# Joint value steps of two key tiles, head parts laid by two transfers each in another order, and less fill, in a two-layer decoder kernel

## The reference

```python
x = x + _L0_attn_ref(_layernorm(x), ...)                        # "own": causal, 1024 keys, keys and values gated
x = x + _L0_xattn_ref(_layernorm(x), ctx_1024, ctx_1024, ...)   # "cross": rotary, causal mask, 154 keys
x = x + _L0_ffn_ref(_layernorm(x), ...)
x = x + _L1_attn_ref(_layernorm(x), ...)                        # "second": no mask, 1024 keys
x = x + _L1_xattn_ref(_layernorm(x), ctx_1024, ctx_1024, ...)   # one wide head, 154 keys
x = x + _L1_ffn_ref(_layernorm(x), ...)                         # 16 experts

scores = jnp.einsum('bhqd,bhkd->bhqk', q, k) / jnp.sqrt(d)      # inside each of the 16-head attentions
w = jax.nn.softmax(scores, axis=-1)
out = jnp.einsum('bhqk,bhkd->bhqd', w, v)
```

## Time and profile before

| | before |
| --- | --- |
| median of 3 runs | 3350.33 us (3348.94 to 3357.76) |
| the profiled execution | 3356.7 us, its span 3355.1 us |
| mean granted clock of PE | 0.996 of full |
| PE busy | 3191.1 us, 95% |
| DVE / ACT / POOL busy | 2323.0 (69%) / 1782.8 (53%) / 634.7 us (19%) |
| transfers | 147.74 MB, mean 44 GB/s |

### The profile page before, as it was taken

The page is one execution under the profiler, slowest core; times in us unless marked ns, Lnnn a source line. Parts: engine busy times, 40 slices in busy tenths (PEclk is TensorE's granted clock), DMA queues, the critical chain, the costliest instruction groups (busy, mean ns, idle before and its releaser), DMA issues.

```text
span 3355.1 us, 46975 instructions
## 1 busy us (share of the span) xinstructions
PE 3191.1 (95%) x17720; PEld 1713.3 (51%) x17720; DVE 2323.0 (69%) x4331; ACT 1782.8 (53%) x2551; POOL 634.7 (19%) x1166
## 2 busy tenths in 40 slices
PE   6999889999999989999999998999999999899999
PEld 4444433378644443337864444334786444433477
DVE  7856688556685578856678557885667855788555
ACT  3565546643456555664355555566424655556632
POOL 0322010024132201012403120100340321020033
PEclk9999999999999999999999999999999999999999
DMA  3212011023121202111312020120231202021023
GB/s 138 51 34 39 1 34 34 11 65 114 32 52 26 40 1 38 30 35 53 115 38 43 18 40 1 39 39 25 63 105 42 40 17 39 5 44 30 10 84 96
DMA packets 118101, 147.74 MB, mean 44 GB/s; under 512 B 25384, under 2 KB 75920, under 8 KB 117596
## 3 DMA queue, kind: packets, MB, share of 16 engines
q1 hardware_dynamic: 117876, 144.74, 18.1%
HBM read 74.25 MB, written 4.46 MB: 23 GB/s over the span
## 4 chain that ended last, share of the span: by engine, by line
PE 51%; DVE 8%; ACT 4%; issue 2%; DMA 1%; SPq 1%; POOL 0%; DVEq 0%; ACTq 0%
PE psum L1908 13%; PE psum L708 9%; PE psum L674 8%; PE psum L646 7%; PE psum L1000 4%; DVE small L796 3%; ACT work L756 2%; PE psum L939 1%; PE psum L717 1%; PE psum L500 1%; DMA work<-work 1%; PE psum L481 1%; PE psum L929 1%; SPq L863 1%; PE psum L1734 1%
## 5 line engine op out<-in xcount | busy, mean ns | idle before, releaser
L796 DVE TENSOR_REDUCE small<-psum 128x1 f32<-128x512 f32 (+6 forms) x1856 | 1136.7, 656 | 210.2 <-PE psum L646 175.9
L756 ACT ACTIVATE work<-psum 128x1024 f32<-128x1024 f32 (+5 forms) x1024 | 918.3, 935 | 419.4 <-PE psum L674 317.4
L646 PE MATMUL psum<-work 96*128 96x512 bf16 (+4 forms) x2688 | 655.7, 308 | 32.8 <-DVE small L796 16.2
L1908 PE MATMUL psum<-rounded_work 128*128 128x512 f32 x2592 | 602.0, 394 | 9.9 <-DVE rounded_work L1994 6.5
L674 PE MATMUL psum<-work 99*128 99x512 bf16 (+4 forms) x2048 | 564.2, 358 | 6.9 <-ACT work L756 4.0
L1908 PEld LDWEIGHTS psum<-rounded_work 128*128 128x128 f32 x2592 | 489.9, 190 | 116.0 <-DVE rounded_work L1994 8.3
L708 PE MATMUL psum<-work 128*32 128x512 f32 (+4 forms) x4480 | 532.3, 528 | 1.6 <-ACT work L756 1.4
L646 PEld LDWEIGHTS psum<-work 96*128 96x128 bf16 x2688 | 233.5, 97 | 544.4 <-DVE small L796 332.2
L674 PEld LDWEIGHTS psum<-work 99*128 99x128 bf16 (+1 forms) x2048 | 178.5, 97 | 199.3 <-ACT work L756 63.1
L2009 ACT CAST rounded_work<-work 128x512 fp32r<-128x512 f32 x144 | 89.4, 621 | 344.5 <-DVE work L2050 321.7
L846 POOL CAST small<-small 128x16 bf16<-128x16 f32 x96 | 18.8, 196 | 1156.2 <-DVE small L803 586.8
(11 more groups left out here) (297 smaller groups left out, 3765.2 us busy)
## 6 DMA issues: line engine op xcount, KB each, us to landing
work<-work SPq DMA_DIRECT2D x320, 192.0 KB, 4.3
work<-combine SPq DMA_DIRECT2D x64, 512.0 KB, 4.1
work<-in_w_gate SPq DMA_DIRECT2D x64, 128.0 KB, 3.5
work<-in_w_up SPq DMA_DIRECT2D x64, 128.0 KB, 3.5
work<-in_w_down SPq DMA_DIRECT2D x64, 128.0 KB, 3.8
work<-in_x SPq DMA_DIRECT2D x8, 512.0 KB, 4.9
out<-x SPq DMA_DIRECT2D x8, 512.0 KB, 2.9
work<-work SPq DMA_DIRECT2D x64, 28.9 KB, 2.0
```

The costliest lines, as they stand in the source:

```text
L646: ins = nc.tensor.matmul(dst[:, c * n:(c + 1) * n], A.q_pair[0:ROWS, slot, h, P * i:P * (i + 1)], A.k_of(pair, h)[0:ROWS, s0:s0 + n], star ...
L756: nc.scalar.activation(probs[0:size, n % 4, :, 0:P * many], banks(2 * (n % 2), 2)[0:size, :, 0:P * many], ACT.Exp, scale=DH ** -0.5).then_ ...
L796: nc.vector.tensor_reduce(tops[:, pair % 2, places[0]:places[-1] + 1:step], src, AX.X, ALU.max) \
L1908: ins = nc.tensor.matmul(dst, a_parts[i], b_parts[j], start=start and n == 0, stop=stop and n == 2, skip_group_check=True)
```

## The change

It has four parts. (a) Values are emitted two key tiles at a time, and there are six `probs` buffers in place of four. (b) A head's stack is laid by two transfers of 48 rows each: one of the three high parts (for the queries read three times from one part), one of the rest; so a stack has one copied part instead of three, the copies move from DVE to ACT and POOL, and a half whose parts are ready may go before the other. Context keys are laid pair by pair like the others, in front of the queries of that pair. (c) Fill is 14 and 2 in place of 26 and 9, and the second stage's ring waits for a unit of its own per bank. (d) `wide_q` is no longer resident; it is loaded in the second stage ahead of pair 6's top transfer.

```diff
+PROBS = 6
-    def value(pair, s):
-        pieces = [("value", pair, s)]
-        if s == len(steps) - 1:
+    def values(pair, s):
+        pieces = [("value", pair, s), ("value", pair, s + 1)]
+        if s + 1 == len(steps) - 1:
...
-            while sum(len(steps[later]) for _, later in held[1:]) >= 2:
-                value(*held.pop(0))
-    for which in held:
-        value(*which)
+            while sum(len(steps[later]) for _, later in held[2:]) >= 2:
+                values(*held[0])
+                held = held[2:]
+    for which in held[::2]:
+        values(*which)
...
-        probs = area.take(4, 2, HALF)
+        probs = area.take(PROBS, 2, HALF)
...
-                by, n, had = {}, 0, [None] * 3
+                by, n, had = {}, 0, [("second_rest", 4 + j) if self.tag == "second" else None for j in range(3)]
...
-        def load_queries(A, pair):
+        UPPER = 3 * DH
+        def load_queries(A, pair, low=None):
...
-                nc.sync.dma_start(A.q_pair[0:ROWS, slot, h, :], q_cut[r + DH * h:r + DH * (h + 1), :, k, :]) \
-                    .then_inc(*up(LOADED[2 * slot + h], A.tag, pair, by=16))
+                src, dst = q_cut[r + DH * h:r + DH * (h + 1), :, k, :], A.q_pair[:, slot, h, :]
+                if low is not True:
+                    nc.sync.dma_start(dst[0:UPPER, :], spread(src[:, Q_HIGH], 1, 3)).then_inc(*up(LOADED[2 * slot + h], A.tag, pair, by=16))
+                if low is not False:
+                    nc.sync.dma_start(dst[UPPER:ROWS, :], src[:, Q_MIDDLE:Q_LOW + 1]).then_inc(*up(LOADED[2 * slot + h], A.tag, pair, by=16))
...
+                for low in (False, True):
+                    keys_ready(0, low)
+                    load_keys(A, 0, low)
+                if a == "cross":
+                    for pair in (1, 2):
+                        load_keys(A, pair)
+                for low in (False, True):
+                    queries_ready(0, low)
+                    load_queries(A, 0, low)
+                for pair in range(1, A.slots):
+                    if pair == 4:
+                        keys_ready(1)
+                        queries_ready(1)
+                    if a == "second" or pair > 2:
+                        load_keys(A, pair)
                     load_queries(A, pair)
...
+                    if a == "second" and pair == PAIRS_OF_HEADS - 2:
+                        for loaded in range(PAIRS_OF_HEADS - SLOTS, PAIRS_OF_HEADS):
+                            for h in range(2):
+                                sp.wait_ge(*at(LOADED[2 * (loaded % SLOTS) + h], a, loaded))
+                        nc.sync.dma_start(wide_q, io["wide_q"]).then_inc(*up("wide_q_landed", by=16))
...
-                nc.sync.dma_start(ctx_stacks[0:ROWS, head, :], ctx_cut[r:r + DH, :, k, :]).then_inc(*up("context_keys_landed", by=16))
...
-            cross_doubles(0)
             cross_rest(3)
-            cross_doubles(1)
...
-            dve.wait_ge(*at("second_rest", "cut", 3))
-            double_queries(nc.vector, 0, "first_doubled", "q", 0)
...
-            busy_tensor(9, 0)
+            busy_tensor(2, 0)
...
-            busy_tensor(26, cross_banks[0])
+            busy_tensor(14, cross_banks[0])
```

More of the change, by code:

```diff
@@ L501, in project @@
             return ins
+        Q_MIDDLE, Q_MIDDLE_TOO, Q_LOW, Q_HIGH = range(4)
+        K_LOW, K_MIDDLE, K_HIGH, K_HIGH_TOO = range(4)
         area = Area(work, words)
@@ L560, in build_program @@
         wide_v = area.take(2, D)
+        wide_q = area.take(KD, D)
         area.at = WIDE_AT
@@ L624, in heads_tensor @@
             a, ring = A.tag, A.ring()
-            entered(pe)
-            busy_tensor(wait, 7)
+            if entered:
+                entered(pe)
+                busy_tensor(wait, 7)
             def take(*piece):
@@ L696, in heads_tensor @@
                                 i0, _, many = A.steps[s][part]
-                                moving = probs[0:size, A.number[(pair, s, part)] % 4, h, 0:P * many]
+                                moving = probs[0:size, A.number[(pair, s, part)] % PROBS, h, 0:P * many]
                                 dst = bank(7)[rows, P * (i0 // 2):P * (i0 // 2 + many)]
@@ L753, in heads_scalar @@
                     act.wait_ge(*at("scored", a, n))
-                    if n >= 4:
-                        act.wait_ge(*at("valued", a, *A.order[n - 4][0:2]))
-                    nc.scalar.activation(probs[0:size, n % 4, :, 0:P * many], banks(2 * (n % 2), 2)[0:size, :, 0:P * many],
+                    if n >= PROBS:
+                        act.wait_ge(*at("valued", a, *A.order[n - PROBS][0:2]))
+                    nc.scalar.activation(probs[0:size, n % PROBS, :, 0:P * many], banks(2 * (n % 2), 2)[0:size, :, 0:P * many],
                                          ACT.Exp, scale=DH ** -0.5).then_inc(*up("prob", a, n))
@@ L854, in heads_gpsimd, with load_keys @@
                     gate_values(key[1])
[L855 to L856 removed]
                 elif kind == "context":
                     context_gpsimd(*key)
[L860 removed]
+        UPPER = 3 * DH
+        def load_queries(A, pair, low=None):
             k, r, slot = pair // 4, 2 * DH * (pair % 4), pair % A.slots
             for h in range(2):
[L863 to L866 removed]
+                src, dst = q_cut[r + DH * h:r + DH * (h + 1), :, k, :], A.q_pair[:, slot, h, :]
[3 more added lines that the diff above has]
+                    nc.sync.dma_start(dst[UPPER:ROWS, :], src[:, Q_MIDDLE:Q_LOW + 1]).then_inc(*up(LOADED[2 * slot + h], A.tag, pair, by=16))
+        def load_keys(A, pair, low=None):
             k, r, slot = pair // 4, 2 * DH * (pair % 4), pair % A.slots
+            cut = ctx_cut if A.tag == "cross" else k_cut
             for h in range(2):
[L869 to L870 removed]
+                src, dst = cut[r + DH * h:r + DH * (h + 1), :, k, :], A.k_of(pair, h)
+                if low is not True:
+                    nc.sync.dma_start(dst[UPPER:ROWS, :], src[:, K_MIDDLE:K_HIGH_TOO + 1]).then_inc(*up(LOADED[2 * slot + h], A.tag, pair, by=16))
+                if low is not False:
+                    nc.sync.dma_start(dst[0:UPPER, :], src[:, K_LOW:K_HIGH + 1]).then_inc(*up(LOADED[2 * slot + h], A.tag, pair, by=16))
         def minus_ones(tag):
@@ L1638, in second_gpsimd @@
             for n, (name, k, half) in enumerate(second_units):
-                if n < 4:
-                    continue
                 _, _, cut, rest, parts = second_parts[name]
-                pool.wait_ge(*at("first_doubled", "q", 0))
-                pool.wait_ge(*at("second_middle", n))
-                nc.gpsimd.tensor_tensor(half_of(cut[:, parts[2]], k, half), raw_half(rest, k, half), half_of(cut[:, parts[1]], k, half), ALU.subtract) \
-                    .then_inc(*up("second_cut", n))
@@ L1661, in second_banks_free @@
-        def second_banks_free(queue):
-            queue.wait_ge(*at("second_rest", 6))
+                if n >= 4:
+                    pool.wait_ge(*at("second_rest", "cut", 3))
+                    pool.wait_ge(*at("second_middle", n))
+                    nc.gpsimd.tensor_tensor(half_of(cut[:, parts[2]], k, half), raw_half(rest, k, half), half_of(cut[:, parts[1]], k, half), ALU.subtract) \
+                        .then_inc(*up("second_cut", n))
+                if name == "k":
+                    pool.wait_ge(*at("second_high", n))
+                    high_again(k_cut, 2 * k + half, "second")
+                else:
+                    pool.wait_ge(*at("second_middle", n))
+                    middle_again(2 * k + half, "second")
@@ new lines, in second_queries, with second_keys @@
+        def second_queries(k, low=True):
+            if low:
+                sp.wait_ge(*(at("second_cut", 7) if k else at("second_rest", "cut", 3)))
+                sp.wait_ge(*at("part_again", "second", "q", 2 * k + 1))
+            else:
+                sp.wait_ge(*at("second_high", 4 * k + 3))
+        def second_keys(k, low=True):
+            sp.wait_ge(*at("part_again", "second", "k", 2 * k + 1))
+            if low:
+                sp.wait_ge(*(at("second_cut", 5) if k else at("second_rest", "cut", 1)))
+            else:
+                sp.wait_ge(*at("second_middle", 4 * k + 1))
```

166 lines of the change are left out of this document (67 added, 99 removed).

## The result

The changed kernel takes 3452.61 us (median of 4 runs, 3445.02 to 3459.0), the kernel before 3353.89 in the same runs (4, 3348.94 to 3357.76): a ratio of 1.0294, with a 95% interval of 1.0266 to 1.0323. That is 99 us slower. 58 us slower was forecast, with a range that ended at 3445, so the sign was right and the size was not. The profiled execution is the fastest of the four; their granted clocks fall as their times rise (0.984, 0.982, 0.981 and 0.978 for 3445.0, 3449.7, 3455.5 and 3459.0 us), so the trace shows less of the clock's part than the median has.

A forecast was written before the change was run, and what follows sets the result against it. PE was taken to bound the kernel, busy 3191.1 of 3355.1 us. Own stage -3.0, cross +7.0 and second stage +10.5 gave +14.5 us a trip, +58 for four: 3408 us, range 3388 to 3435 (0.8 between 3343 and 3445).

The forecast's parts named there:

- cross entry: Before the first cross score: half-stack issues on SP's queue make it +3 us later a trip, bounds -3 to +7.7.
- the cross stage behind it: After the first cross score: +1.7 us a trip for extra issues at pairs 6 and 7, +2.3 for later tops.
- own stage: Own stage: joint values save 7.3 us, stalls, tail and entry take some back; net -3.0 a trip, bounds -7.3 and +1.
- the second stage's entry: Entry of the second stage: copies leave DVE and half stacks go early, -2.4 us a trip, bounds -3 and 0.
- a rival of 0.13: Whole kernel: more idle PE lowers its clock, or both unknowns lie at their upper ends; 3435 to 3470 us, chance 0.13.
- I take 0.53 and 0.45: SP's queue before the first cross score: assumed us per query half and small key half, 17.1 us for 34 issues.
- the upper end: Cross entry: if a half costs 0.65 us whatever its size, 34 take 22.1 and the first score moves +7.7.
- Second stage: Second stage: stalls after double value blocks +8.1 us, tail +2.9, entry -2.4, wide_q +1.9; +10.5 a trip.
- The 3.02 us from top to score: Second stage: time from a top to a score needing its rows; the plan leaves 2.1, so the top's cycle grows 0.83.
- the recurrence: Second stage: hand-worked double cycle in which first passes wait for DVE's maxima; 5.85 us, not 5.43, +0.18 against now.
- wide_q: Second stage: the 256 KB wide_q transfer ahead of the last but one top costs +1.9 us a trip.
- the first passes wait for DVE over 100 us: Sign in the changed profile: first passes wait for DVE over 100 us in all instead of 16.2.

The follow-up runs named there:

- e5: The changed kernel with 60 fill matmuls in place of 10 ahead of the first cross score; 3424.8 us, 1.0207 of the kernel before.
- e1: The changed kernel with the context keys of pairs 3 to 5 issued early, with those of pairs 1 and 2; 3414.1 us, 1.0173 of the kernel before.
- e8: The changed kernel with the upper query halves of cross pairs 1 and 2 laid by three transfers of 16 rows in place of one of 48; 3463.0 us, one run.
- e3: The changed kernel with value steps one key tile at a time as before; 3392.6 us, 1.0110 of the kernel before.
- e7: The changed kernel with DVE's maxima in the second stage taken over half of each block's columns; 3411.6 us, one run.
- e12: The changed kernel with both DVE's maxima and ACT's exponentials halved in the second stage; 3379.2 us, one run.
- e9: The changed kernel with the fill of before, 26 and 9 matmuls in place of 14 and 2; 3453.9 us, 1.0283 of the kernel before.
- e2: The changed kernel with context keys of pairs 3 to 5 early and queries of pairs 4 and 5 behind tops 0 and 1; 3390.1 us, 1.0101 of the kernel before.
- e6: The changed kernel with each top three first passes into the next pair in place of four; 3514.2 us, one run.

## Why the prediction was wrong in size

Against the sum's terms the two traces have, in us a trip, +4.2 at the cross entry, +4.3 in the cross stage behind it, +2.7 in the own stage, +0.5 at the second stage's entry, -3.0 in the second stage and -1 in the rest: +31 in all, to which the medians add some 10.

- **The clock: the step that failed.** The sum has the wait before the first cross score and nothing for what the clock does behind it. That stood apart, as a rival of 0.13 whose range, 3435 to 3470, is where the result came. The evidence for leaving it out was a window in which PE waited a little at each first pass and kept its clock; this wait was of another kind, 10.8 us without any work, and PE ran at half clock for 23, 16, 4 and 16 us behind it. e5, which fills the wait and changes nothing else, gave 28 us back and came to 3424.8, inside the forecast's range. My text had a wait of some 5 us there and said that it is more than any now; by e1, where waits of 2.6 to 3.5 us were enough, that wait had to have its price too. In the stretch behind the first cross score, where the sum had +4, e5's three trips at full clock show +2.4 to +2.8 and the changed kernel's mean is +8.1.
- **Cross entry: a term mis-sized.** "I take 0.53 and 0.45" for the issues of a half: they are 0.635 each, and e8 has the same for 16 rows. With it the sum gives 21.6 and the upper end, which is what came: +7.2 for +3, 17 us in all. I had reasoned from bytes and rows; the row of the context stacks, 0.65 each for a seventh of the data, said already that an issue of little data is hardly cheaper. The Trainium skill's rule that two transfers to disjoint halves of the partitions are not worth making ("DMA: Bandwidth & Descriptors", section "Rules for kernel authors") fits the outcome: twice the issues, each at 0.635. Whether the halves also serialize, no run here shows. e1, which takes twelve issues out of the way and leaves the clock at half, came to 3414.1, also inside the range: the miss is this term and the clock together.
- **Second stage: the mechanism right, the size too large.** Forecast +0.18 for each plain cycle, +0.09 with the spin, +0.83 with the top; measured +0.13 and +0.20 (5.80 and 5.87), +0.02, and +0.70 (6.68); a pair +1.03 for +1.28, a cycle of the tail 5.03 for 5.02. e3 took all of it back. The 3.02 us from top to score held other work of PE and was only an upper bound of the chain; it is 2.89. What the recurrence missed was ACT's chain beside DVE's, of nearly the same length (e7, e12); it changed no number. With `wide_q` and the tail the sum had +12.9 a trip and +9.9 came: these 12 us in all, by luck, hid a part of the miss.
- **Own stage: mis-sized.** -3.0 forecast, -0.3 measured, 11 us in all. A pair is 15.64 us for 15.88, 0.24 less where four joints less 0.5 leave 0.4; 0.23 more of wait for ACT's gather before the spin (0.30 for 0.07) is a part of that. The first pair is 0.4 longer and the stretch behind the last first pass too, where +1 was taken. The rest was not taken apart.
- **wide_q:** +1.9 forecast; the score behind top 6 waits 1.44 to 1.61 us where those of other pairs wait 0.70 to 0.77, and its pair is 0.7 to 0.9 longer (0.6 to 0.8 in e3). In two trips of the four the clock fell behind it and cost 1.7 more.
- **Signs in the profile:** "the first passes wait for DVE over 100 us" was wrong, 23.7. The stall is real but lies mostly in matmuls that follow one another 0.1 to 0.2 later than their work. "Idle before" does not measure a loss that is made of such pieces; the distance between two value blocks does. The lower clock was named among what would make the forecast wrong, and it did.

## What to carry to other kernels

Merging two steps of a pipelined order saves what lies between them, and takes away cover from every chain that ran beside the single steps: look at the buffers between the engines and the longer gap before merging (that more of them would have held the gain was not tried). In a queue, count issues, not bytes, and look at which later transfer stands behind them. A wait of TensorE can have a price behind it as well: if a long one can't be removed, fill it, and judge the fill by the clock of the stretch after it.

## What the runs showed of the hardware

- A transfer's issue on SP took 0.59 us and the next one stood 0.635 after it, with 16 rows of 2 KB, 48 rows of 2 KB, or 48 rows of 308 bytes (the changed kernel, e8). 96 rows of 308 bytes took 0.65 and 96 rows of 2 KB 1.06.
- The granted clock fell to its lower level (0.50, 1.2 GHz) during or right behind the waits before the first cross score, of 8.5 to 11.1 us (the changed kernel, e3, e9) and of 2.6 to 3.5 us (e1), in every trip. Shorter waits between busy stretches did it in some trips and not in others: 1.52 and 2.37 us but not 1.24 and 1.17 (e2), 1.28 but not 1.18 (e5), two of four of 1.44 to 1.61 (the changed kernel, top 6), 13 of 28 of 1.30 to 1.65 (e6).
- Behind the same late first score the clock came back after 23, 16, 4 and 16 us of work in the changed kernel, after 8 to 9 us in each trip of e3, with single steps. Why is not settled.
